# ScalarE writes all stored states into the scans' inputs, and VectorE multiplies two of four chunks of dt and x

## What is computed

```python
xc = silu(conv(x @ W_in) + b_conv)            # 512 channels
dt = softplus(dt_low @ W_dt.T + b_dt)
def step(h, inp):                              # 16 states a channel
    h = h * exp(dt_t[:, :, None] * A) + (dt_t * u_t)[:, :, None] * B_t[:, None, :]
    y = einsum('bdn,bn->bd', h, C_t)
y = (ys + xc * D) * silu(z)
```

## Time and profile before

| | |
|---|---|
| median of 3 runs | 2131.1 us (2129.78 to 2132.01) |
| the profiled execution | 2130.74 us, span 2128.9 us |
| busy: VectorE, TensorE, GpSimd, ScalarE | 92%, 87%, 85%, 71% of the span |
| scans of the 16 steps | from 81.5 to about 1675 us |
| granted TensorE clock, mean | 0.916 |

### The profile page before, as it was taken

How to read it: one execution, slowest core, us unless ns; L and a number is a source line. 1 busy time by engine, 2 the same in 40 slices (tenths; PEclk the granted TensorE clock), 3 DMA queues, 4 the chain that set the end, 5 groups by cost and what they waited for, 6 DMA issues and landing times.

```text
span 2128.9 us, 24092 instructions
## 1 busy us (share of the span) xinstructions
PE 1857.0 (87%) x6364; PEld 793.2 (37%) x6364; DVE 1954.3 (92%) x1807; ACT 1520.2 (71%) x3144; POOL 1806.6 (85%) x622
## 2 busy tenths in 40 slices
PE   7879898989889898989897988889876699999997
PEld 3323232323233323333232323233322266656564
DVE  7999999999999999999999999999999876657776
ACT  5787779797988888786879797888876344424443
POOL 5689999999999999999999999999999533425544
PEclk9999898989898998989898989899878799999999
DMA  7836445453536253545445353626252663235554
GB/s 264 251 105 165 103 118 125 110 130 102 129 93 158 74 146 95 142 109 131 114 118 124 102 129 102 140 83 156 70 126 63 224 258 110 90 91 87 89 85 73
DMA packets 140071, 265.20 MB, mean 125 GB/s; under 512 B 21232, under 2 KB 43760, under 8 KB 138784
## 3 DMA queue, kind: packets, MB, share of 16 engines
q1 hardware_dynamic: 125344, 241.92, 42.4%
q0 software_dynamic: 13296, 17.80, 4.9%
q10 hardware_dynamic: 1296, 3.93, 0.5%
HBM read 194.38 MB, written 70.26 MB: 124 GB/s over the span
## 4 chain that ended last, share of the span: by engine, by line
PE 31%; POOL 31%; issue 15%; ACT 12%; DVE 8%; DMA 1%; POOLq 0%; DVEq 0%; SPq 0%; ACTq 0%
POOL hst L933 21%; POOL dbu L921 7%; PE psum L2239 6%; PE psum L2175 5%; ACT psum L1247 5%; PE psum L2018 5%; DVE hst L1598 4%; PE psum L2258 3%; PE psum L2187 3%; POOL dt L913 2%; PE psum L1966 2%; PE psum L1938 2%; PE psum L1950 1%; DVE dbu L1577 1%; PE psum L2003 1%
## 5 line engine op out<-in xcount | busy, mean ns | idle before, releaser
L933 POOL TENSOR_TENSOR hst<-hst,c_rep 128x2048 f32<-128x2048 f32 x254 | 1153.4, 4606 | 3.7 <-ACT state L1233 3.6
L1598 DVE TENSOR_TENSOR_SCAN hst<-psum,state,dbu 128x1024 f32<-128x1024 f32 x384 | 879.4, 2331 | 7.7 <-ACT psum L1247 7.6
L1247 ACT ACTIVATE psum<-dt_rep,neg_a 128x512 f32<-128x512 f32 (+1 forms) x1024 | 659.8, 676 | 136.7 <-DVE hst L1598 131.0
L1577 DVE TENSOR_TENSOR dbu<-psum,b_rep 128x2048 f32<-128x2048 f32 x176 | 398.7, 2265 | 10.1 <-PE psum L2003 10.1
L921 POOL TENSOR_TENSOR dbu<-dtu_rep,b_rep 128x2048 f32<-128x2048 f32 x80 | 369.3, 4616 | 9.5 <-DMA dtu_rep<-dtu_scratch 4.9
L2018 PE MATMUL psum<-hst,same 128*32 128x512 f32 x2048 | 284.8, 706 | 81.5 <-POOL hst L933 74.3
L2003 PE MATMUL psum<-dt,same 32*128 32x512 f32 x352 | 216.5, 697 | 91.2 <-DVE dbu L1577 86.1
L1598 DVE TENSOR_TENSOR_SCAN hst<-psum,dbu 128x1024 f32<-128x1024 f32 x128 | 286.1, 2272 | 9.6 <-ACT psum L1247 9.5
L1950 PE MATMUL psum<-xp,taps 128*128 128x512 f32 x512 | 237.1, 606 | 3.9 <-ACT sp_tmp L1216 3.9
L1042 POOL DMA_INDIRECT out_x<-h,target_u x71 | 110.9, 1562 | 131.9 <-DVE h L1868 57.1
L2018 PEld LDWEIGHTS psum<-hst,same 128*32 128x32 f32 x2048 | 68.1, 127 | 304.7 <-issue 170.9
(11 more groups left out here) (183 smaller groups left out, 2504.9 us busy)
## 6 DMA issues: line engine op xcount, KB each, us to landing
dt_rep<-dt_scratch SPq DMA_DIRECT2D x256, 256.0 KB, 4.8
dtu_rep<-dtu_scratch SPq DMA_DIRECT2D x320, 64.0 KB, 1.9
taps<-taps_scratch SPq DMA_DIRECT2D x64, 256.0 KB, 4.5
b_rep<-bc_scratch SPq DMA_DIRECT2D x64, 256.0 KB, 5.0
c_rep<-bc_scratch SPq DMA_DIRECT2D x64, 256.0 KB, 7.8
dt_scratch<-dt SPq DMA_DIRECT2D x63, 256.0 KB, 5.6
h<-slot_scratch SPq DMA_DIRECT2D x71, 129.5 KB
sp_tmp<-t_scratch SPq DMA_DIRECT2D x16, 512.0 KB, 6.9
```

The lines of the kernel that those rows point to most:

```text
L933: nc.gpsimd.tensor_tensor(h, h, c_rep[q % 2][:], ALU.mult).then_inc(prod_done, 1)
L1247: nc.scalar.activation(psum[:, PS_A + i, kept], dt_rep[:, G % 2, j, kept], ACT.Exp, scale=neg_a[:, q % 2, u, i:i + 1]).then_inc(exp_done, 1)
L1577: nc.vector.tensor_tensor(dbu[:, U % DBU, :, :], psum[:, PS_U:PS_U + 1, :].broadcast_to((P, NG, TB)), b_rep[U // UNITS % 2][:], ALU.mult). ...
L1598: nc.vector.tensor_tensor_scan(both(hst[:, U % RING, groups, :]), both(psum[:, PS_A + 2 * pair:PS_A + 2 * pair + 2, :]), both(dbu[:, U % D ...
```

## The change

In a seeded unit ScalarE now adds the stored state to the first input of all four groups: two seeds ahead of the first pair of decays and two ahead of the second, where there were two in all. Every scan begins from the constant 0.0. The four `first_decay` instructions of a chunk move from n = 1 to n = 3 of the unit ahead of it. For chunks 1 and 2 of every step but the first, the product of dt and x goes from GpSimd to VectorE, which reads dt from the PSUM bank; ScalarE copies that dt to `sp_tmp` (for the store to DRAM) instead of `dt`, counts it in `dt_kept`, and leaves the bank for VectorE to free.

```diff
+VECTOR_CHUNKS = (1, 2)
+EARLY_INPUT_AT, LATE_INPUT_AT = 12, 13
...
+def by_vector(q, c):
+    return q > 0 and c in VECTOR_CHUNKS
...
 def seeds(U):
-    return 2 * sum(seeded(u) for u in range(U + 1))
+    return NG * sum(seeded(u) for u in range(U + 1))
...
             def store_dt(q, c):
-                drained(sp, "sum", q, c)
+                if by_vector(q, c):
+                    sp.wait_ge(dt_kept, vector_copies(q, c))
+                else:
+                    drained(sp, "sum", q, c)
...
# GpSimd
-                if t == (0 if q > 0 else 2):
+                if T == 2:
                     step_input(q, 2)
...
-                if t == 14 and ahead:
-                    step_input(q + 1, 1)
...
# ScalarE
             def copy_dt(q, c):
                 bank, free = filled(act, "sum", q, c)
-                nc.scalar.activation(dt[:, c, :], psum[:, bank, :], ACT.Copy).then_inc(free, 1)
+                if by_vector(q, c):
+                    nc.scalar.activation(sp_tmp[:, c, :], psum[:, bank, :], ACT.Copy).then_inc(dt_kept, 1)
+                else:
+                    nc.scalar.activation(dt[:, c, :], psum[:, bank, :], ACT.Copy).then_inc(free, 1)
...
-                    if n == 0 and seeded(T):
-                        for pair in range(2):
-                            seed(T, pair)
+                    if n % 2 == 0 and seeded(T):
+                        for i in range(n, n + 2):
+                            seed(T, i)
...
-                    if n == 1 and t % GN == GN - 1 and T + 1 < ALL_UNITS and seeded(T + 1):
+                    if n == 3 and t % GN == GN - 1 and T + 1 < ALL_UNITS and seeded(T + 1):
                         first_decays((T + 1) // GN)
...
# VectorE
+            def step_input(q, c):
+                bank, free = filled(dve, "sum", q, c)
+                dve.wait_ge(xc_done, q + 1)
+                dve.wait_ge(dt_kept, vector_copies(q, c))
+                nc.vector.tensor_tensor(dtu[:, c, :], psum[:, bank, :], xc[:, q % 2, c, :], ALU.mult).then_inc(free, 1)
...
-                start = state[:, q % 2, u, 2 * pair + q % 2, :] if seeded(U) else 0.0
...
-                    both(dbu[:, U % DBU, groups, :]), start, ALU.mult, ALU.add).then_inc(scan_done, 2)
+                    both(dbu[:, U % DBU, groups, :]), 0.0, ALU.mult, ALU.add).then_inc(scan_done, 2)
...
             for T in range(ALL_UNITS):
                 q, t = divmod(T, UNITS)
+                if t == EARLY_INPUT_AT and q + 1 < STEPS:
+                    step_input(q + 1, 1)
                 if T + 1 < ALL_UNITS and not on_pool(T + 1):
                     multiply(T + 1)
...
                 scan(T, 0)
...
+                if t == LATE_INPUT_AT and q + 1 < STEPS:
+                    step_input(q + 1, 2)
```

More of the change, by code:

```diff
@@ L119, in on_pool, with vector_copies, pool_inputs @@
     return U % UNITS in POOL_UNITS
+def by_vector(q, c):
+    return q > 0 and c in VECTOR_CHUNKS
+def vector_copies(q, c):
+    return sum(by_vector(k, j) for k in range(q + 1) for j in range(NC) if (k, j) <= (q, c))
+def pool_inputs(q, c):
+    return sum(not by_vector(k, j) for k in range(q + 1) for j in range(NC) if (k, j) <= (q, c))
 def vector_mults(U):
@@ L412, in mixer_and_experts @@
         dtu_done = sem("dtu_done")
+        dt_kept = sem("dt_kept")
         u_full = sem("u_full")
@@ L528, in mult_ready, with input_ready @@
                 eng.wait_ge(vector_mult_done, vector_mults(U))
+        def input_ready(eng, q, c):
+            if by_vector(q, c):
+                drained(eng, "sum", q, c)
+            else:
+                eng.wait_ge(dtu_done, pool_inputs(q, c))
         def dbu_free(eng, U):
@@ L628, in store_dt @@
             def store_dt(q, c):
-                drained(sp, "sum", q, c)
+                if by_vector(q, c):
+                    sp.wait_ge(dt_kept, vector_copies(q, c))
+                else:
+                    drained(sp, "sum", q, c)
                 if q >= 2:
                     sp.wait_ge(dt_loaded[c % 2], 16 * GN * ((NC * (q - 2) + c) // 2 + 1))
-                sp.dma_start(dt_dram[q % 2, c].rearrange("j d t -> (j d) t"), dt[:, c, :]).then_inc(dt_stored[c % 2], 16)
+                src = sp_tmp if by_vector(q, c) else dt
+                sp.dma_start(dt_dram[q % 2, c].rearrange("j d t -> (j d) t"), src[:, c, :]).then_inc(dt_stored[c % 2], 16)
             def spread_dt(q, c):
@@ L647, in store_dtu @@
                 n = pool_mults(UNITS * q + u)
-                sp.wait_ge(dtu_done, NC * q + c + 1)
+                input_ready(sp, q, c)
                 if n > 2:
@@ L673, in load_sum @@
                         sp.wait_ge(h_stored[n], 16)
+                after = min(q + 1, STEPS - 1)
                 for c in range(2):
-                    drained(sp, "sum", min(q + 1, STEPS - 1), c)
+                    drained(sp, "sum", after, c)
+                    if by_vector(after, c):
+                        sp.wait_ge(dt_stored[c % 2], 16 * ((NC * after + c) // 2 + 1))
                 sp.dma_start(t_blk, t_dram[block_of(q)]).then_inc(t_loaded, 16)
@@ L1212, in softplus @@
                     act.wait_ge(bc_stored, 16 * (q + 1))
+                if by_vector(q - 1, c):
+                    act.wait_ge(dt_stored[c % 2], 16 * ((NC * (q - 1) + c) // 2 + 1))
                 bank, free = filled(act, "dt", q, c)
@@ L1265, in first_decays @@
                 if seeded_chunks(G) > 0:
-                    act.wait_ge(seed_done, 2 * GN * seeded_chunks(G))
+                    act.wait_ge(seed_done, NG * GN * seeded_chunks(G))
                 for j in range(GN):
@@ L1269, in first_decays, with seed @@
                                          scale=dt_rep[:, G % 2, j, at:at + 1]).then_inc(first_decay_done, 1)
-            def seed(U, pair):
+            def seed(U, i):
                 q, u = divmod(U, UNITS)
-                i, at = 2 * pair + 1 - q % 2, first_of(q)
+                at = first_of(q)
                 act.wait_ge(first_decay_done, GN * (seeded_chunks(U // GN) + 1))
@@ L1587, in scan @@
                     mult_ready(dve, U)
-                    if seeded(U):
-                        dve.wait_ge(seed_done, seeds(U))
                     if U >= RING:
                         dve.wait_ge(chunk_summed, (U - RING) // GN + 1)
+                if seeded(U):
+                    dve.wait_ge(seed_done, seeds(U) - 2 * (1 - pair))
                 if u == 0:
@@ L1998, in spread_input @@
                 if j == 0 or (j == 1 and on_pool(U - 1)):
-                    pe.wait_ge(dtu_done, G + 1)
+                    input_ready(pe, *divmod(G, NC))
                 if U > 0:
```

## The result

The changed kernel takes 2205.7 us (median of 4 runs, 2204.91 to 2206.89) against 2131.2 of before; the ratio is 1.0351, 95% interval 1.0335 to 1.0366. It is 74.5 us slower; 2208 were forecast.

What follows compares the result with a forecast made beforehand. GpSimd was taken as the bound at 99.24 us a step, VectorE within 1%. Eight steps of 105.3, three of 104.4, three of 102.1, with +6 and -1 at the ends, gave +77.5 on 2130.7: 2208 us, range 2165 to 2235.

Steps and rivals of the forecast that it cites:

- The step that carried it: Unit 12: VectorE's chunk 1 product waits for ScalarE's copy, itself behind decays awaiting unit 11's second scan; at least 2.5 us.
- ScalarE's queue from the scan of unit 8 to the end of the copy: ScalarE's work ahead of chunk 1's copy: 20.8 us before, plus four added seed pairs at 0.55, so 23.0 us.
- the estimate of 0.38: Price of a seed pair on ScalarE by the skill's table; the forecast used the trace's 0.55, else some 11 us lower.
- The wait in the steps that seed and save: VectorE before chunk 1's product, steps 2 to 5 and 10 to 13: 23.0 - 16.8 = 6.2 us a step.
- The wait in the other steps: VectorE before chunk 1's product: 5.3 us in steps 6, 7, 14; 3.3 in steps 1, 8, 9; 7.3 in step 0.
- The step lengths: Eight steps of 105.3 us, three of 104.4 and three of 102.1, against 99.24 before.
- The product of VectorE: Each 128x512 product of dt and xc from PSUM on VectorE takes 0.6 us, like the gating product; two a step, 1.2.
- The product for chunk 2: Between unit 13's scans it waits for the copy at (13, 3): VectorE arrives after 11.6 us, copy after 11.2; just hidden.
- GpSimd: 92% of a step: GpSimd loses two products a step, stops being the bound, and falls to some 92% of a step, with waits for scans.
- Other late decays: Added seeds delay decays that VectorE's scans await, 0.55 us at each of two places: 1.1 us a step.

Runs made afterwards that it cites:

- the square of runs: Changed kernel's product 1 ahead of unit 12 or behind its first scan: with two seeds a unit 2188.3 or 2131.3 us, with four 2205.7 or 2148.2.
- the run without the first state: Against the kernel before: VectorE takes chunk 2's product alone, seeds unchanged, all scans start from 0.0, first group's stored state left out; 2114.3 us, 0.9925.

## Why the prediction was right

The step that carried it, a wait of VectorE's first product for a copy that stands behind decays which stand behind VectorE's own last scan, is shown by the trace (15 waits, 80.6 us) and by the square of runs: 57 us go with the place alone. By its terms:

- ScalarE's queue from the scan of unit 8 to the end of the copy: 23.0 us forecast, 22.95 measured. The added pairs of seeds at 0.55 are right; the estimate of 0.38 from the table of the Trainium skill ("VectorE: DVE Perf Modes", TRN2 errata), named beside the sum, is not what the trace shows.
- The wait in the steps that seed and save: 6.2 forecast, 5.55 measured. The first scan of unit 11 waited 0.98 instead of 0.3 for its decays and so used up the difference: VectorE came that much later to the product. The two terms together were 6.5, and 6.53 measured.
- The wait in the other steps: 5.3 forecast for steps 6, 7 and 14, 5.9, 5.4 and 4.6 measured; in steps 1, 8 and 9, which have no seeds, 3.3 forecast and 4.1 measured. There the old trace's whole distance of 4.1 stayed: I took 0.8 off for ScalarE's wait for TensorE ahead of the copy of chunk 0, and that wait is still there (1.6, 2.0 and 2.1 us). In step 0 the wait was 7.9, 7.3 forecast. All 15 waits come to 80.6 us, by the forecast's terms to 82.7; that these lie so close is in part luck, since the errors have opposite signs.
- The step lengths: 105.3, 104.4 and 102.1 forecast. Three steps of the first kind took 317.1/3 = 105.7, two of the last 204.6/2 = 102.3. In the first kind VectorE is busy for 98.25 us instead of 97.7, so its own work was put 0.5 too low; in the last kind the wait of 4.1 instead of 3.3 was made up for by VectorE's other waits, 0.4 instead of 1.1. The mean over 13 steps is 104.74 against 104.4 in the forecast's sum over 14.
- The product of VectorE: 0.6 taken from the gating; 581.84 to 582.44, 0.60.
- The product for chunk 2 hides, as the margin of 0.4 us said: only the 15 early products wait. With the early one moved behind a scan, it does wait a little (0.1 to 0.4 us); the cover was the stall itself.
- GpSimd: 92% of a step forecast, 291.02/317.10 = 92% measured, waiting for scans.
- Other late decays: 1.1 us a step forecast, at units 6 and 8. It was 0.8 at unit 8 in the steps that seed and save, and 0.07 at unit 6, where the kernel before had waited 0.3 to 2.8 in ten steps. Right in size, wrong in one of two places. Why the wait of unit 6 went is not shown: with VectorE's products alone it went altogether, with the added seeds alone in most steps, and in both GpSimd is no longer full.

What I mis-sized otherwise only showed in the experiments: how little of the seeds' price a relieved VectorE can absorb. By the prediction's own terms a seeded step without the new wait is 97.7 + 0.3 + 1.1 = 99.1 us, no longer than before. The changed kernel with its wait all but moved away takes 2148.2, 17 us more than before, and the seeds alone 2144.4 where 2128 to 2142 were expected, since units 12 and 13 are late too.

So where did the intended gain go? VectorE's scans did shorten (9 us by the run without the first state) and GpSimd was relieved. The first is given back nearly four times over, where chunk 2 alone is on VectorE, by seeds on an engine that was late at the soft-plus groups. The second is worth only the distance to VectorE, which stood within 1% of it: 8 us with one product moved, and nothing with two.

## What to carry to other kernels

Before an instruction is moved to another engine, follow the queue of whoever feeds it back to the last thing that it waits for: if that is the moved instruction's own predecessor, the wait is built in, its length is what stands between in that queue, and no slack on average helps. Where three engines are this level, averages (ScalarE 85% busy) say nothing of such places; the distances between two rows in the old trace do, even though nobody waits there yet. And before a copy is moved forward, look where its producer gets its bank.

## What the runs showed that was not expected

GpSimd's weighting of 128x2048 has a mean duration of 4606 ns in the kernel before and 4531 to 4565 ns in all the others, 1.4% less (4544 against 4606) for an instruction of identical form. One might take that for 1 us of time a step. It isn't: from start to start, which is what counts in a queue without idle time, nothing changed. In the kernel before, and then in the run without the first state (4535 ns in the mean):

```profile
555.47 13.57 POOL L933 TENSOR_TENSOR hst<-hst,c_rep 128x2048 f32<-128x2048 f32 x3
568.92 1.35 POOL L913 TENSOR_TENSOR dt<-dt,xc 128x512 f32<-128x512 f32 x1
...
418.26 9.01 POOL L969 TENSOR_TENSOR hst<-hst,c_rep 128x2048 f32<-128x2048 f32 x2
427.23 1.26 POOL L949 TENSOR_TENSOR dt<-dt,xc 128x512 f32<-128x512 f32 x1
```

(568.92 - 555.47)/3 = 4.48 us and (427.23 - 418.26)/2 = 4.49 us. Only the overlap of one record with the next differs. VectorE's records do the same: scans with a stored state last 2331 ns in the mean before and 2366 in three steps of the run with chunk 2 alone, and both follow each other at 2.25 us. Being full does not explain it either: in the run without the first state GpSimd is busy for 196.64 of 197.00 us. No run here tells why. A mean duration is no price until the distance between starts has been read beside it.
